# Softmax attention on one core: the values of a key tile in one piece of 512 queries, with both maxima and all scores between two pieces

## The chip, the cores and the metric

The kernel runs on one core of a Trainium2 chip. The metric is the device time of one execution in microseconds (us). Before the change it is 3828.96 us, the median of three runs (3827.2 to 3834.28). Engines are named as in the profile: PE is TensorE's matrix multiply, PEld its weight load, DVE is VectorE, ACT is ScalarE, POOL is GpSimd, SP is SyncE, which here only issues DMAs.

## The reference, cut to what matters

Two transformer layers on x of 2 x 2048 tokens by 256 channels. Each has a modulated layer norm, an attention and a mixture of experts. Two pieces are full softmax attentions over 2048 tokens with 16 heads of 16 channels, and they take two thirds of the time: the attention of layer 0, and the attention inside the second block of layer 1.

```
# layer 0 (q and k with rotary position, weights W_q, W_k, W_v)
scores = jnp.einsum('blhd,bshd->bhls', q, k) / math.sqrt(D_HEAD)
weights = jax.nn.softmax(scores, axis=-1)
out = jnp.einsum('bhls,bshd->blhd', weights, v).reshape(B, L, D_MODEL)
...
# layer 1, second block
attn = jnp.einsum('bqhd,bkhd->bhqk', q, k) / jnp.sqrt(jnp.asarray(hd, x.dtype))
attn = jax.nn.softmax(attn, axis=-1)
attn_out = jnp.einsum('bhqk,bkhd->bqhd', attn, v).reshape(B, S, D)
```

Everything else (projections, router and experts of layer 0, linear attention and experts of layer 1) is not touched.

## The kernel before

`softmax_attention` is called once in each layer. Both calls run the same program. The outer loop `it` goes over the two batches. Inside, `j` goes over 16 query blocks: four groups of four heads, times four blocks of 512 queries. Inside a block, `u` goes over 16 key tiles of 128 keys. So there are 2 x 2 x 16 = 64 query blocks and 64 x 16 = 1,024 key tiles in all.

In a key tile four kinds of work meet.

- Scores (L758): for each head h = 0 to 3 of the group one matmul makes the scores of 128 keys (output partitions) by 512 queries. Head h uses rows 0 to 63 or 64 to 127 of the array, so two heads' matmuls run side by side. The result goes to one of three PSUM banks (`SB = 3`), taken in turn over all scores.
- Exponentials (L823): ScalarE takes each bank to `probs`, which has two buffers by the parity of u. One instruction a head.
- Values (L772): four heads' matmuls, 17 columns of weights each (16 channels and a column of ones for the sum), at output partitions 32h. They add into one PSUM bank, `o_ps`, over the 16 tiles. A matmul in full fp32 appears in the trace as two passes, so four matmuls are eight records. They work one tile behind the scores: in tile u the values of u - 1 are made.
- Maxima (L740 and L844): the softmax is shifted by the row maximum, which needs scores with queries on the partitions. TensorE makes these for the next query block (eight tiles ahead, `LEAD`), two units a tile. A unit is a pair of matmuls, 128 queries by 1024 keys, into one of two PSUM slots (`max_ps`); VectorE reduces it with one instruction (L844). I call the two units of a tile M0 and M1.

The order on TensorE is written out by hand. A tile is two equal rounds: the first half of the values (queries 0 to 255), scores h = 2 and 3, M0; then the second half of the values, the next tile's scores h = 0 and 1, M1. TensorE waits at these places:

- scores c wait until exponential c - 3 is done (L756: `exp_done` at c - SB + 1), because they use its bank;
- a unit of maxima waits until the reduction of the unit two before it is done (L736: `slot_taken`);
- the first half of the values waits for the four exponentials of its tile (L764), and for u = 0 also for VectorE to have turned the result of the last query block out of `o_ps` (L766: `o_copied`).

VectorE, in its own hand-written order (L860 to L874), takes the maxima as they come. After the first unit of a block it turns the last block's result (`turn_result`, L849, a transpose out of `o_ps`, which waits for the last values of that block). After the first unit of tile 2 it divides (L853, L856). In tiles 8 and 9 it reduces and turns the row maxima (L381 to L394), which SyncE stores and loads as the shift of the next block.

The names and lines that the rest speaks of: scores L750 to L759, values L761 to L776, the tile's order L784 to L816, the exponentials L818 to L838, VectorE L840 to L875. TensorE, ScalarE, VectorE and SyncE are bound together by semaphores only.

Of the kernel before, what the change touches and what calls it, by code (L numbers as in the profile page):

```python
# [26 lines left out]
G = 512  # L27
TPG = G // P
GPB = T // G
KH = D // P  # L30
HG = 4
NHG = NH // HG
AUG = HD + 1
# [284 lines left out]
NB = GPB * NHG  # L318
LEAD = 8
MAXI = HG * TPG * 2  # L320
FIRST = MAXI + 2 * LEAD
# [23 lines left out]
def maximum_parts(k):  # L345

    return k // (TPG * GPB), k // GPB % TPG, k % GPB
# [249 lines left out]
NG = NHG  # L597
KT = TPB
# [7 lines left out]
def softmax_attention(nc, m, io, ai, tag, zero_slots=False, last=False):  # L606
# [5 lines left out]
    with ExitStack() as ctx:  # L612
        sb, pb, sem = allocators(ctx, nc, tag)
        q_sb, k_sb = ai.q, [ai.k[0], sb("k_sb1", [P, PAIRS, T], F32R)]
        v_sb = sb("v_sb", [P, 2, TPB, VROW])
        probs = sb("probs", [P, 2, HG, G])
# [20 lines left out]
        EXPS = KT * HG  # L637
        SLOTS_IT = NB * MAXI
# [84 lines left out]

        @block.tensor
        def _(pe):
            def maxima(used, r, j, k, it2):


                if k == 0:
                    pe.wait_ge(q_loaded[j % QR], NQ * (it2 * (NB // QR) + j // QR + 1))  # L730
                    if j % GPB == 0:
                        g = j // GPB
                        if g == 1:
                            pe.wait_ge(rows_set, 4)
                        pe.wait_ge(k_loaded[g % 2], NK * (it2 * (NG // 2) + g // 2 + 1))
                pe.wait_ge(slot_taken, used - 1)  # L736
                pair, tile, part = maximum_parts(k)
                for half in range(2):
                    rows = slice(half * HROWS, half * HROWS + XROWS)
                    last = nc.tensor.matmul(max_ps[:, r, half], q_sb[rows, j % QR, pair, tile * P:(tile + 1) * P],  # L740
                                            k_sb[j // GPB % 2][rows, pair, part * G:(part + 1) * G], start=True, stop=True)
                    if half == 0:
                        yield
                last.then_inc(slot_ready, 1)
                yield

            def scores(n, j, u, h, first=False):
                c = n * EXPS + u * HG + h
                if u == 0 and h == 0:
                    pe.wait_ge(shift_stored, NSH * (n + 1))  # L750
                if j == 0 and u == 0 and h < SB:

                    if h == 0 and not first:
                        pe.wait_ge(exp_done, n * EXPS)
                else:
                    pe.wait_ge(exp_done, c - SB + 1)  # L756
                pair, rows = h // 2, slice(h % 2 * HROWS, h % 2 * HROWS + XROWS)
                nc.tensor.matmul(s_ps[:, (j * EXPS + u * HG + h) % SB], k_sb[j // GPB % 2][rows, pair, u * P:(u + 1) * P],  # L758
                                 q_sb[rows, j % QR, pair], start=True, stop=True).then_inc(s_ready, 1)  # L759

            def values(n, j, u, it, part):  # L761

                if part == 0:
                    pe.wait_ge(exp_done, n * EXPS + (u + 1) * HG)  # L764
                    if u == 0:
                        pe.wait_ge(o_copied, n)  # L766
                        if j % GPB == 0:
                            g = j // GPB
                            pe.wait_ge(v_loaded[g % 2], 16 * (it * (NG // 2) + g // 2 + 1))
                cols = slice(part * (G // 2), (part + 1) * (G // 2))  # L770
                for h in range(HG):
                    last = nc.tensor.matmul(o_ps[32 * h:32 * h + AUG, cols], v_sb[:, j // GPB % 2, u, h * AUG:(h + 1) * AUG],  # L772
                                            probs[:, u % 2, h, cols], start=(u == 0 and part == 0), stop=(u == KT - 1),
                                            skip_group_check=True)
                if part == 1:
                    last.then_inc(pv_done, 1)  # L776

            pe.wait_ge(o_zeroed, 1)
            for h in range(2):
                scores(0, 0, 0, h, first=True)  # L780
            with pe.Fori(0, NIT) as it:
                for j in range(NB):
                    n = it * NB + j
                    for u in range(KT):  # L784

                        def ahead(i):
                            k, slot = 2 * (u + LEAD) + i, slot_of(j, u, i)
                            g = j + 1 + k // MAXI
                            return maxima(FIRST + it * SLOTS_IT + slot, slot % 2, g % NB, k % MAXI, it + g // NB)
# [7 lines left out]
                        def values_behind(part):  # L797

                            if u > 0:
                                values(n, j, u - 1, it, part)  # L800
                            elif j > 0:
                                values(n - 1, j - 1, KT - 1, it, part)

                        a, b = ahead(0), ahead(1)
                        values_behind(0)
                        scores(n, j, u, 2)
                        scores(n, j, u, 3)
                        next(a)
                        next(a)
                        values_behind(1)  # L810
                        next_scores(0)
                        next_scores(1)
                        next(b)
                        next(b)
                for part in range(2):
                    values(n, NB - 1, KT - 1, it, part)  # L816

        @block.scalar  # L818
        def _(act):
# [20 lines left out]
        @block.vector  # L840
        def _(dve):
            def max_take(used, r, j, k):
                dve.wait_ge(slot_ready, used + 1)  # L843
                nc.vector.reduce_max(part_max[:, j % 2, k], max_ps[:, r], AX.X).then_inc(slot_taken, 1)  # L844

            def turn_result(n):
                dve.wait_ge(pv_done, (n + 1) * KT)
                dve.wait_ge(o_ready, n)  # L848
                nc.vector.transpose(o_sb[:].rearrange("p k c -> p (k c)"), o_ps[:]).then_inc(o_copied, 1)  # L849

            def divide(n, j):
                dve.wait_ge(o_copied, n + 1)
                nc.vector.reciprocal(inv[:], o_sb[:, :, HD]).then_inc(inv_ready, 1)  # L853
                dve.wait_ge(inv_ready, n + 1)
                dve.wait_ge(o_stored, (n - 1 if j > 1 else n - j) * 16 * HG)
                nc.vector.tensor_tensor(o_div[:, j % 2], o_sb[:, :, 0:HD], inv[:].unsqueeze(2).broadcast_to([P, G // 32, HD]),  # L856
                                        ALU.mult).then_inc(o_ready, 1)

            nc.vector.memset(o_ps[:], 0.0).then_inc(o_zeroed, 1)  # L859
            with dve.Fori(0, NIT) as it:  # L860
                for j in range(NB):
                    n = it * NB + j
                    for u in range(KT):
                        for i in range(2):
                            k, slot = 2 * (u + LEAD) + i, slot_of(j, u, i)
                            max_take(FIRST + it * SLOTS_IT + slot, slot % 2, j + 1 + k // MAXI, k % MAXI)
                            if u >= KT - LEAD:
                                row_maxima(nc, dve, ai, n + 1, j + 1, k % MAXI, slots_until(it, j, KT - LEAD - 1, 1))
                            if j > 0 and u == 0 and i == 0:
                                turn_result(n - 1)  # L870
                            if j > 0 and u == RESULT_AT and i == 0:
                                divide(n - 1, j - 1)
                turn_result(n)
                divide(n, NB - 1)  # L874
            dve.wait_ge(slot_taken, FIRST + NIT * SLOTS_IT)  # L875
# [1099 lines left out]
```

## Time and profile before

| | |
|---|---|
| median of three runs | 3828.96 us |
| the profiled execution, its own time | 3825.79 us |
| its span | 3824.0 us |
| TensorE busy | 3496.8 us (91%) |
| VectorE busy | 3312.5 us (87%) |
| ScalarE busy | 2525.3 us (66%) |
| GpSimd busy | 253.1 us (7%) |
| clock granted to TensorE, mean | 0.953 of full speed |
| DMA, mean over the span | 53 GB/s |

The profile shows one execution. The shares of busy time are means over stages with different limits. The two attentions lie from about 215 to 1508 us and from about 2514 to 3806 us; nearly all of the maxima, exponentials, scores and values of the table of groups lie there. The start of a matmul record is the start of its weight load when that load was not hidden, and its end is modelled; two records can overlap. So the distance from one start to the next tells more than the length of a record. The clock is a share of 2.4 GHz: 1.00 is 2.4 GHz, 0.50 is 1.2 GHz.

### The profile page before, as it was taken

Reading aid. Unit: us, or ns where it says so; the run is one execution under the profiler, and the core shown is the slowest. Engines: PE = TensorE matmul, PEld = TensorE weight load, DVE = VectorE, ACT = ScalarE, POOL = GpSimd, SP = SyncE. Lnnn points to the kernel's source line nnn. Section 1 sums busy time; section 2 is a strip of 40 time slices with the busy share of each in tenths; the row PEclk is TensorE's granted clock in tenths of the full one; section 3 lists DMA queues with packets and bytes.
Section 4 is the critical chain, followed back from the end, with each engine's and each line's share of the span. In section 5 each row is a group of like instructions: output and inputs, shape, how many; then the busy total and the mean of one; then the engine's idle time right before and its main releaser. Section 6 shows DMA issues by size and latency. Waiting matters only on the chain. (4 is left out here: it accounts for less than half of the span.)

```text
span 3824.0 us, 89676 instructions
## 1 busy us (share of the span) xinstructions
PE 3496.8 (91%) x30116; PEld 1598.4 (42%) x30116; DVE 3312.5 (87%) x4392; ACT 2525.3 (66%) x4636; POOL 253.1 (7%) x211
## 2 busy tenths in 40 slices
PE   6889999999999998676888799889999999999997
PEld 4433333333333333565666577533333333333332
DVE  5989999999999997524666587899999999999997
ACT  2268888888888886232222223158888888888886
POOL 2210000000000000232210000000000010000001
PEclk8879999999999999898999899889999999999999
DMA  5840220202202022253000233220220212202021
GB/s 170 196 128 14 42 36 18 38 14 41 38 14 42 14 40 62 97 169 95 27 22 11 66 78 76 64 40 14 42 36 18 38 42 58 37 14 42 14 52 43
DMA packets 281193, 200.93 MB, mean 53 GB/s; under 512 B 203785, under 2 KB 234930, under 8 KB 275644
## 3 DMA queue, kind: packets, MB, share of 16 engines
q1 hardware_dynamic: 272300, 166.30, 20.3%
q0 software_dynamic: 8496, 29.43, 2.3%
q8 instruction: 237, 3.88, 0.4%
q14 instruction: 160, 1.31, 0.1%
HBM read 114.29 MB, written 81.82 MB: 51 GB/s over the span
## 5 line engine op out<-in xcount | busy, mean ns | idle before, releaser
L844 DVE TENSOR_REDUCE att_in_part_max<-att_l_max_ps 128x2 f32<-128x1024 f32 x2048 | 2447.3, 1218 | 50.5 <-PE att_l_max_ps L740 49.5
L823 ACT ACTIVATE att_l_probs<-att_l_s_ps 128x512 f32<-128x512 f32 x4096 | 2222.9, 595 | 345.9 <-PE att_l_s_ps L758 89.9
L772 PE MATMUL att_l_o_ps<-att_l_probs,att_l_v_sb 128*17 128x256 f32 x16384 | 1289.4, 387 | 49.1 <-DVE att_l_o_sb L849 39.2
L772 PEld LDWEIGHTS att_l_o_ps<-att_l_probs,att_l_v_sb 128*17 128x17 f32 x16384 | 273.7, 95 | 791.0 <-ACT att_l_probs L823 406.2
L758 PE MATMUL att_l_s_ps<-att_in_q_sb,att_in_k_sb 50*128 50x512 f32 x2052 | 522.0, 503 | 16.9 <-DVE att_l_o_ps L859 8.2
L758 PE MATMUL att_l_s_ps<-att_in_q_sb,att_l_k_sb 50*128 50x512 f32 x2048 | 511.7, 496 | 0.0
L740 PE MATMUL att_l_max_ps<-att_in_k_sb,att_in_q_sb 50*128 50x512 f32 x2048 | 414.7, 399 | 0.0
L740 PE MATMUL att_l_max_ps<-att_l_k_sb,att_in_q_sb 50*128 50x512 f32 x2048 | 403.4, 389 | 0.0
L758 PEld LDWEIGHTS att_l_s_ps<-att_in_q_sb,att_in_k_sb 50*128 50x128 f32 x2052 | 195.1, 185 | 459.9 <-ACT att_l_probs L823 438.2
L758 PEld LDWEIGHTS att_l_s_ps<-att_in_q_sb,att_l_k_sb 50*128 50x128 f32 x2048 | 190.6, 183 | 434.1 <-ACT att_l_probs L823 434.1
L740 PEld LDWEIGHTS att_l_max_ps<-att_in_k_sb,att_in_q_sb 50*128 50x128 f32 x2048 | 197.3, 189 | 2.0
L740 PEld LDWEIGHTS att_l_max_ps<-att_l_k_sb,att_in_q_sb 50*128 50x128 f32 x2048 | 193.9, 186 | 3.1 <-issue 0.7
L1859 DVE SCALAR_TENSOR_TENSOR ffn_acc<-ffn_qk_ps,ffn_comb,ffn_acc 128x256 f32<-128x256 f32 x256 | 123.9, 484 | 32.8 <-PE ffn_qk_ps L1768 25.2
L1356 DVE TENSOR_TENSOR post_hid<-post_act_gate,post_zT_ps 128x256 f32<-128x256 f32 x32 | 13.5, 421 | 105.5 <-ACT post_act_gate L1252 105.5
L1768 PE MATMUL ffn_qk_ps<-ffn_w_hi,ffn_h_hi 128*128 128x512 f32 x256 | 102.4, 400 | 0.0
L717 POOL TENSOR_TENSOR att<-att,all_gates 128x1024 f32<-128x1024 f32 x8 | 18.9, 2365 | 1249.7 <-DMA att<-att_rows 1249.7
L1768 PE MATMUL ffn_qk_ps<-ffn_w_hi,ffn_h_lo 128*128 128x512 f32 x256 | 101.3, 396 | 0.0
L1768 PE MATMUL ffn_qk_ps<-ffn_w_lo,ffn_h_hi 128*128 128x512 f32 x256 | 101.0, 394 | 0.0
L1626 DVE TENSOR_TENSOR lin_masked<-lin_qk_ps,all_triu 128x1024 f32<-128x1024 f32 x64 | 75.0, 1213 | 24.4 <-PE lin_qk_ps L1463 24.4
L1245 ACT ACTIVATE post_slot_hT<-post_y_ps,all_modv 128x256 f32<-128x256 f32 x64 | 32.6, 560 | 85.9 <-PE post_y_ps L1149 85.8
L823 ACT ACT_TABLE_LOAD x4 | 5.1, 1283 | 121.9 <-PEq L71 118.6
L1558 ACT ACTIVATE lin_o_sb<-lin_o_ps 128x512 f32<-128x512 f32 x32 | 19.1, 597 | 98.5 <-PE lin_o_ps L1472 98.5
(218 smaller groups left out, 2791.4 us busy)
## 6 DMA issues: line engine op xcount, KB each, us to landing
att_in_q_sb<-q_hi SPq DMA_DIRECT2D x280, 64.0 KB
att_in_k_sb<-k_hi SPq DMA_DIRECT2D x40, 256.0 KB, 9.4
att_in_q_sb<-q_lo SPq DMA_DIRECT2D x140, 72.0 KB
att_l_v_sb<-v_rows SPq DMA_DIRECT2D x18, 544.0 KB, 14.0
att_l_k_sb<-k_hi SPq DMA_DIRECT2D x32, 256.0 KB, 9.1
slot_rows<-att_l_zeros POOLq DMA_DIRECT2D x8, 1024.0 KB, 13.9
att_rows<-att_l_o_div SPq DMA_DIRECT2D x256, 32.0 KB, 1.8
post_rows<-slot_rows SPq DMA_DIRECT2D x32, 256.0 KB, 2.9
```

The costliest lines, as they stand in the source:

```text
L717: nc.gpsimd.tensor_tensor(att, att, gate, ALU.mult).then_inc(att_scaled, 1)
L740: last = nc.tensor.matmul(max_ps[:, r, half], q_sb[rows, j % QR, pair, tile * P:(tile + 1) * P], k_sb[j // GPB % 2][rows, pair, part * G:( ...
L758: nc.tensor.matmul(s_ps[:, (j * EXPS + u * HG + h) % SB], k_sb[j // GPB % 2][rows, pair, u * P:(u + 1) * P], q_sb[rows, j % QR, pair], sta ...
L772: last = nc.tensor.matmul(o_ps[32 * h:32 * h + AUG, cols], v_sb[:, j // GPB % 2, u, h * AUG:(h + 1) * AUG], probs[:, u % 2, h, cols], star ...
L823: nc.scalar.activation(probs[:, u % 2, h], s_ps[:, (j * EXPS + u * HG + h) % SB], ACT.Exp, scale=float(HD) ** -0.5).then_inc(exp_done, 1)
L844: nc.vector.reduce_max(part_max[:, j % 2, k], max_ps[:, r], AX.X).then_inc(slot_taken, 1)
L1245: nc.scalar.activation(slot_hT[:, i % 2, half], rT_ps[:, i % 2, half], ACT.Identity, bias=m.modv[:, 0, 2, half, b:b + 1], scale=m.modv[:, ...
L1356: nc.vector.tensor_tensor(hid[:, i % 2], act_gate[:, i % 2], gf_ps[:, i % 2, 1], ALU.mult).then_inc(hid_ready, 1)
L1558: nc.scalar.activation(o_sb[:], o_ps[:], ACT.Copy).then_inc(o_copied, 1)
L1626: nc.vector.tensor_tensor(masked[:, t % 2, banks].rearrange("p r e n -> p (r e) n"), qk_ps[:, banks].rearrange("p r (e n) -> p (r e) n", n=P),
L1768: last = nc.tensor.matmul(qk_ps[:, pair], h[:, slot * KH + kh, t * P:(t + 1) * P], w[:, kh, pair * 2 * D:(pair + 1) * 2 * D], start=(kh == ...
L1859: nc.vector.scalar_tensor_tensor(acc[:, t], qk_ps[:, e // 2, (e % 2) * D:(e % 2 + 1) * D], comb[:, t, e:e + 1], acc[:, t], ALU.mult, ALU.a ...
```

## The change

On TensorE the tile has one round instead of two. The values of the tile before are made in one piece of 512 queries: four matmuls instead of two times four. The order is scores h = 2 and 3; values; next tile's scores h = 0 and 1; M0; M1. So both maxima and all four scores stand between two pieces of values. The start flag of the accumulation is on the one piece now. The generator that issued a unit of maxima in two steps becomes a plain function.

On VectorE `turn_result` goes ahead of the first unit of maxima of a block instead of behind it. Everything else stays: the three score banks, the two slots, the number of instructions on ScalarE and VectorE, the DMAs and what the waits ask for.

```diff
-            def values(n, j, u, it, part):
-
-                if part == 0:
-                    pe.wait_ge(exp_done, n * EXPS + (u + 1) * HG)
...
-                cols = slice(part * (G // 2), (part + 1) * (G // 2))
+            def values(n, j, u, it):
+                pe.wait_ge(exp_done, n * EXPS + (u + 1) * HG)
+                if u == 0:
+                    pe.wait_ge(o_copied, n)
...
                 for h in range(HG):
-                    last = nc.tensor.matmul(o_ps[32 * h:32 * h + AUG, cols], v_sb[:, j // GPB % 2, u, h * AUG:(h + 1) * AUG],
-                                            probs[:, u % 2, h, cols], start=(u == 0 and part == 0), stop=(u == KT - 1),
-                                            skip_group_check=True)
-                if part == 1:
-                    last.then_inc(pv_done, 1)
+                    last = nc.tensor.matmul(o_ps[32 * h:32 * h + AUG], v_sb[:, j // GPB % 2, u, h * AUG:(h + 1) * AUG],
+                                            probs[:, u % 2, h], start=(u == 0), stop=(u == KT - 1))
+                last.then_inc(pv_done, 1)
...
-                        a, b = ahead(0), ahead(1)
-                        values_behind(0)
                         scores(n, j, u, 2)
                         scores(n, j, u, 3)
-                        next(a)
-                        next(a)
-                        values_behind(1)
+                        if u > 0:
+                            values(n, j, u - 1, it)
+                        elif j > 0:
+                            values(n - 1, j - 1, KT - 1, it)
                         next_scores(0)
                         next_scores(1)
-                        next(b)
-                        next(b)
-                for part in range(2):
-                    values(n, NB - 1, KT - 1, it, part)
+                        for i in range(2):
+                            maxima(i)
+                values(n, NB - 1, KT - 1, it)
...
+                            if j > 0 and u == 0 and i == 0:
+                                turn_result(n - 1)
                             max_take(FIRST + it * SLOTS_IT + slot, slot % 2, j + 1 + k // MAXI, k % MAXI)
                             if u >= KT - LEAD:
                                 row_maxima(nc, dve, ai, n + 1, j + 1, k % MAXI, slots_until(it, j, KT - LEAD - 1, 1))
-                            if j > 0 and u == 0 and i == 0:
-                                turn_result(n - 1)
```

The instructions of TensorE for one key tile in the middle of a block, before, from one first half of the values on: `o_ps` is the result, `s_ps` the scores, `max_ps` the maxima; 17x256 is one head's values.

```order
L772 MATMUL att_l_o_ps<-att_l_probs,att_l_v_sb 17x256 x4
L758 MATMUL att_l_s_ps<-att_in_q_sb,att_in_k_sb 128x512
L756 REGISTER_ALU
L758 MATMUL att_l_s_ps<-att_in_q_sb,att_in_k_sb 128x512
L736 REGISTER_ALU
L740 MATMUL att_l_max_ps<-att_in_k_sb,att_in_q_sb 128x512 x2
L772 MATMUL att_l_o_ps<-att_l_probs,att_l_v_sb 17x256 x4
L756 REGISTER_ALU
L758 MATMUL att_l_s_ps<-att_in_q_sb,att_in_k_sb 128x512
L756 REGISTER_ALU
L758 MATMUL att_l_s_ps<-att_in_q_sb,att_in_k_sb 128x512
```

The same place after:

```order
L740 MATMUL att_l_max_ps<-att_in_k_sb,att_in_q_sb 128x512 x2
L753 REGISTER_ALU
L755 MATMUL att_l_s_ps<-att_in_q_sb,att_in_k_sb 128x512
L753 REGISTER_ALU
L755 MATMUL att_l_s_ps<-att_in_q_sb,att_in_k_sb 128x512
L766 MATMUL att_l_o_ps<-att_l_probs,att_l_v_sb 17x512 x4
L753 REGISTER_ALU
L755 MATMUL att_l_s_ps<-att_in_q_sb,att_in_k_sb 128x512
L753 REGISTER_ALU
L755 MATMUL att_l_s_ps<-att_in_q_sb,att_in_k_sb 128x512
L736 REGISTER_ALU
L740 MATMUL att_l_max_ps<-att_in_k_sb,att_in_q_sb 128x512 x2
```

In the second list the scores h = 2 and 3 (the first two rows of L755) follow a pair of maxima, the four value matmuls of 512 columns follow them, and the next scores h = 0 and 1 stand ahead of the maxima. The halves of the values are gone from between scores h = 0 and 1 and scores h = 2 and 3.

The instructions of VectorE where one block ends and the next begins, before: the reduction is a unit of maxima, the transpose is the turn of the result.

```order
L844 TENSOR_REDUCE att_in_part_max<-att_l_max_ps 128x2
L843 REGISTER_ALU
L844 TENSOR_REDUCE att_in_part_max<-att_l_max_ps 128x2
L847 REGISTER_ALU
L849 STREAM_TRANSPOSE att_l_o_sb<-att_l_o_ps 128x512
L843 REGISTER_ALU
L844 TENSOR_REDUCE att_in_part_max<-att_l_max_ps 128x2
```

After:

```order
L830 TENSOR_REDUCE att_in_part_max<-att_l_max_ps 128x2
L829 REGISTER_ALU
L830 TENSOR_REDUCE att_in_part_max<-att_l_max_ps 128x2
L833 REGISTER_ALU
L835 STREAM_TRANSPOSE att_l_o_sb<-att_l_o_ps 128x512
L829 REGISTER_ALU
L830 TENSOR_REDUCE att_in_part_max<-att_l_max_ps 128x2
```

The transpose stood behind the first reduction of the new block; now it stands ahead of it.

## Rows read from the trace of the kernel before

**Rows 1.** Busy time of each engine in attention stretches (windows; us, then busy and count)

```profile
core 0: us, PE busy (x) PEld busy (x) DVE busy (x) ACT busy (x) POOL busy (x), PEclk, DMA share, GB/s
300.00:800.00 500.00, 489.35 (x4816) 174.39 (x4812) 493.53 (x501) 435.06 (x802) 0.00 (x0) 1.00 0.17 29
...
3200.00:3700.00 500.00, 489.36 (x4816) 174.44 (x4812) 493.51 (x501) 435.05 (x802) 0.00 (x0) 1.00 0.17 29
```

**Rows 2.** Groups by line; busy us, mean ns, idle us before and its releaser

```profile
L844 DVE TENSOR_REDUCE att_in_part_max<-att_l_max_ps 128x2 f32<-128x1024 f32 x2048 | 2447.3, 1218 | 50.5 <-PE att_l_max_ps L740 49.5
...
L772 PE MATMUL att_l_o_ps<-att_l_probs,att_l_v_sb 128*17 128x256 f32 x16384 | 1289.4, 387 | 49.1 <-DVE att_l_o_sb L849 39.2 <-ACT att_l_probs L823 9.9
...
L849 DVE STREAM_TRANSPOSE att_l_o_sb<-att_l_o_ps 128x512 f32<-128x512 f32 x64 | 45.1, 705 | 0.0
```

**Rows 3.** Timeline, TensorE, one undisturbed round; start us, us, engine, line

```profile
1038.93 0.62 PE L772 MATMUL att_l_o_ps<-att_l_probs,att_l_v_sb 128*17 128x256 f32 x8
...
1039.49 0.50 PE L758 MATMUL att_l_s_ps<-att_in_q_sb,att_l_k_sb 50*128 50x512 f32 x2
...
1039.83 0.40 PE L740 MATMUL att_l_max_ps<-att_l_k_sb,att_in_q_sb 50*128 50x512 f32 x2
...
1040.15 0.63 PE L772 MATMUL att_l_o_ps<-att_l_probs,att_l_v_sb 128*17 128x256 f32 x8
```

**Rows 4.** Timeline, VectorE, division and the reductions behind it

```profile
1035.30 0.24 DVE L853 RECIPROCAL att_l_inv<-att_l_o_sb 128x16 f32<-128x16 f32 x1
...
1036.02 4.61 DVE L844 TENSOR_REDUCE att_in_part_max<-att_l_max_ps 128x2 f32<-128x1024 f32 x4
```

**Rows 5.** Timeline, all engines, around a turn of the result

```profile
1029.60 0.70 DVE L849 STREAM_TRANSPOSE att_l_o_sb<-att_l_o_ps 128x512 f32<-128x512 f32 x1
...
1030.41 0.62 PE L772 MATMUL att_l_o_ps<-att_l_probs,att_l_v_sb 128*17 128x256 f32 x8 [0.78 <-ACT att_l_probs L823]
...
1030.96 0.50 PE L758 MATMUL att_l_s_ps<-att_in_q_sb,att_l_k_sb 50*128 50x512 f32 x2
...
1031.30 0.39 PE L740 MATMUL att_l_max_ps<-att_l_k_sb,att_in_q_sb 50*128 50x512 f32 x2
...
1031.50 1.08 ACT L823 ACTIVATE att_l_probs<-att_l_s_ps 128x512 f32<-128x512 f32 x2 [0.98 <-PE att_l_s_ps L758]
...
1031.73 1.22 DVE L844 TENSOR_REDUCE att_in_part_max<-att_l_max_ps 128x2 f32<-128x1024 f32 x1 [0.32 <-PE att_l_max_ps L740]
```

**Rows 6.** Chain of waits, two turns, one query block apart; start us, us

```profile
2719.15 0.71 DVE att_l_o_sb L849
...
2759.02 0.71 DVE att_l_o_sb L849
```

**Rows 7.** Timeline, TensorE, matmuls of 512 and of 256 columns (projection)

```profile
94.76 6.60 PE L581 MATMUL qkv_qk_ps<-qkv_ln_hT,qkv_w_qk 128*128 128x512 f32 x15
...
102.08 3.62 PE L588 MATMUL qkv_v_ps<-qkv_w_v,qkv_ln_hT 128*128 128x256 f32 x16
```

**Rows 8.** Instructions of three lines; duration ns min/median/max, first and last start

```profile
L823 ACT ACTIVATE att_l_probs<-att_l_s_ps x4096: 592/597/618, 216.7 to 3800.6; 128x512 f32<-128x512 f32 x196
...
L758 PE MATMUL att_l_s_ps<-att_in_q_sb,att_in_k_sb x2052: 387/497/793, 215.9 to 3801.3; 50*128 50x512 f32 x187
...
L740 PE MATMUL att_l_max_ps<-att_l_k_sb,att_in_q_sb x2048: 383/386/502, 323.2 to 3741.6; 50*128 50x512 f32 x187
```

**Rows 9.** Timeline, start of the second attention, all engines

```profile
2515.55 1.57 ACT L823 ACTIVATE att_l_probs<-att_l_s_ps 128x512 f32<-128x512 f32 x3
...
2516.20 0.79 PE L758 MATMUL att_l_s_ps<-att_in_q_sb,att_in_k_sb 50*128 50x512 f32 x1 [0.26 <-ACT att_l_probs L823]
```

**Rows 10.** Windows of the first maxima of layer 1 (line L362)

```profile
2460.00:2470.00 10.00, 7.15 (x18) 2.59 (x18) 10.00 (x9) 0.00 (x0) 0.00 (x0) 0.50 0.00 0
```

**Rows 11.** Timeline, TensorE, second attention, clock at half

```profile
2520.46 1.05 PE L772 MATMUL att_l_o_ps<-att_l_probs,att_l_v_sb 128*17 128x256 f32 x8
...
2522.60 0.96 PE L772 MATMUL att_l_o_ps<-att_l_probs,att_l_v_sb 128*17 128x256 f32 x8
```

More of the change, by code:

```diff
@@ L725, in _, with maximum @@
         def _(pe):
-            def maxima(used, r, j, k, it2):
+            def maximum(used, r, j, k, it2):
                 if k == 0:
@@ L741, in maxima @@
                                             k_sb[j // GPB % 2][rows, pair, part * G:(part + 1) * G], start=True, stop=True)
-                    if half == 0:
-                        yield
                 last.then_inc(slot_ready, 1)
-                yield
             def scores(n, j, u, h, first=False):
@@ L759, in scores @@
                                  q_sb[rows, j % QR, pair], start=True, stop=True).then_inc(s_ready, 1)
-            def values(n, j, u, it, part):
-                if part == 0:
-                    pe.wait_ge(exp_done, n * EXPS + (u + 1) * HG)
[L765 to L769, printed above, removed]
-                cols = slice(part * (G // 2), (part + 1) * (G // 2))
-                for h in range(HG):
-                    last = nc.tensor.matmul(o_ps[32 * h:32 * h + AUG, cols], v_sb[:, j // GPB % 2, u, h * AUG:(h + 1) * AUG],
-                                            probs[:, u % 2, h, cols], start=(u == 0 and part == 0), stop=(u == KT - 1),
-                                            skip_group_check=True)
-                if part == 1:
-                    last.then_inc(pv_done, 1)
+            def values(n, j, u, it):
+                pe.wait_ge(exp_done, n * EXPS + (u + 1) * HG)
+                if u == 0:
+                    pe.wait_ge(o_copied, n)
+                    if j % GPB == 0:
+                        g = j // GPB
+                        pe.wait_ge(v_loaded[g % 2], 16 * (it * (NG // 2) + g // 2 + 1))
+                for h in range(HG):
+                    last = nc.tensor.matmul(o_ps[32 * h:32 * h + AUG], v_sb[:, j // GPB % 2, u, h * AUG:(h + 1) * AUG],
+                                            probs[:, u % 2, h], start=(u == 0), stop=(u == KT - 1))
+                last.then_inc(pv_done, 1)
             pe.wait_ge(o_zeroed, 1)
@@ L784, in _, with maxima @@
                     for u in range(KT):
-                        def ahead(i):
+                        def maxima(i):
                             k, slot = 2 * (u + LEAD) + i, slot_of(j, u, i)
                             g = j + 1 + k // MAXI
-                            return maxima(FIRST + it * SLOTS_IT + slot, slot % 2, g % NB, k % MAXI, it + g // NB)
+                            maximum(FIRST + it * SLOTS_IT + slot, slot % 2, g % NB, k % MAXI, it + g // NB)
                         def next_scores(h):
@@ L795, in next_scores @@
                                 scores(n + 1, (j + 1) % NB, 0, h)
[L797 to L802, printed above, removed]
-                        a, b = ahead(0), ahead(1)
-                        values_behind(0)
                         scores(n, j, u, 2)
                         scores(n, j, u, 3)
-                        next(a)
-                        next(a)
-                        values_behind(1)
+                        if u > 0:
+                            values(n, j, u - 1, it)
+                        elif j > 0:
+                            values(n - 1, j - 1, KT - 1, it)
                         next_scores(0)
                         next_scores(1)
-                        next(b)
-                        next(b)
-                for part in range(2):
-                    values(n, NB - 1, KT - 1, it, part)
+                        for i in range(2):
+                            maxima(i)
+                values(n, NB - 1, KT - 1, it)
         @block.scalar
```

## The prediction

> **What bounds the kernel now.** I began with the clock and the busy time by engine. Inside both attention stages the clock is granted in full (1.00), TensorE is busy 98% of the time and VectorE 99% [rows 1]. Which of two full engines is the bound can't be told by their shares. So I went to the groups by line: the maxima on VectorE (L844) have 50 us of idle before them over 2,048 instructions, the values (L772) 49 us, so neither waits much [rows 2]. Then the timeline of a stretch without disturbance [rows 3]. TensorE repeats values, scores, maxima every 1.22 us: values at 1038.93, again at 1040.15. A key tile is two such rounds, 2.44 us. The steps in a round are values to scores 0.56, scores to maxima 0.335 (0.34 in the row), maxima to values 1.22 - 0.56 - 0.335 = 0.33.
>
> VectorE can go faster than that. After its reciprocal and division it catches up: four reductions in 4.61 us, with 1.22 for the last, are (4.61 - 1.22) / 3 = 1.13 us apart [rows 4]. ScalarE too: after a wait two exponentials cover 1.08 us, so the second starts 0.49 us after the first (1.08 less 0.59), about 2 us for a tile of four [rows 5]. So TensorE's own sequence is the bound in the undisturbed tile, and VectorE follows 7% below it.
>
> A query block (16 key tiles) takes 39.87 us between two turns of the result (L849) [rows 6]. 32 rounds of 1.22 are 39.04; the other 0.83 is the turn itself. There TensorE stands 0.78 us until VectorE has turned the old result, because the first values of the next block are at the front of the tile [rows 5]; the row puts the wait down to ScalarE, but the turn ended last, at 1029.60 + 0.70 = 1030.30. There are 64 such blocks in the two layers (64 turns in [rows 2]).
>
> **What the change takes off TensorE.** The eight value matmuls in two pieces of 256 columns become four of 512. Each is run in two passes. A pass of full precision costs (6.60 - 0.59) / 14 = 0.43 us for 512 columns and (3.62 - 0.38) / 15 = 0.22 us for 256 [rows 7], so the columns cost what they did: 0.21 more for each of two passes. Saved is what lies between kinds. Values to scores becomes 0.56 + 0.43 = 0.98, once. Scores to maxima stays 0.335. The steps maxima to maxima and maxima to scores have the weights loaded behind the matmul before them: 0.335 less the 0.11 by which a score matmul (0.497) is longer than a maximum matmul (0.386) [rows 8] is 0.23 each. Scores to values is 0.33, as maxima to values was. The sum is 0.98 + 0.335 + 0.23 + 0.23 + 0.33 = 2.10 us a tile against 2.44. If nothing waited, VectorE would be the next bound.
>
> The Trainium skill (TensorEngine Tiling (Array Packing), Key Properties) says that a change of tiling mode drains TensorE. The steps of [rows 3] agree: about 0.1 us more at each change of kind. By that rule alone the tile gains, since it has two changes instead of four; this is the fourth rival below.
>
> **What the change adds: a longer ring of waits.** There are three score banks for four heads. So the fourth scores of a tile, h=3, write the bank that exponential h=0 of the same tile has to have read (L756). The scores h=0 of a tile are issued in the tile before. In the old order one half of the values stood between scores h=3 and the next scores h=0, the other half between scores h=0 and scores h=3. Now nothing but maxima stands between h=0 and h=3, and the whole of the values between h=3 and the next h=0. The ring, from one scores h=0 to the next:
> - scores h=0 start to exponential h=0 start: 1030.96 to 1031.50, 0.535 us [rows 5];
> - the exponential: 0.597 us (median) [rows 8];
> - its end to the weights of the waiting scores: 2515.55 + 0.60 = 2516.15, scores at 2516.20: 0.05 us [rows 9];
> - scores h=3, which now load their weights after the wait and not behind another matmul, to values: 0.33 + 0.11 = 0.435;
> - values to scores h=0: 0.98.
>
> That is 2.60 us a tile, of which 1.18 us pass from h=0 to h=3, where TensorE needs only 0.335 + 0.23 + 0.23 = 0.80. TensorE so stands about 0.4 us in each tile. In the old order the same ring closes in a round: 0.535 + 0.597 + 0.05 = 1.18 against the 1.22 that TensorE takes from one pair of scores to the next: 0.04 us of cover, and the change takes it.
>
> Is anything later than 2.60? VectorE needs 2 x 1.13 = 2.26. Its two slots: M0 starts 0.335 after scores h=0; its reduction starts 0.43 later (1031.30 to 1031.73, [rows 5]), at 0.77; the second at 1.90, and ends at 3.12 with the 1.22 us of L844. The next M1 can start at 3.12 + 0.05 = 3.17, if VectorE is heard as soon as ScalarE is. That is 0.57 after the next scores h=0 at 2.60. It may be as late as 1.18 - 0.335 = 0.84 without holding scores h=3. So there is 0.27 us of slack in each tile.
>
> **Once in a block.** The turn now goes ahead of the first maxima on VectorE and waits for the last values of the block. These start at 1.18 + 0.435 = 1.61 after scores h=0, and the second pass ends about 1.0 later, at 2.65, while VectorE has maxima to reduce until 1.90 + 1.13 = 3.03. The turn takes 0.70 us, to 3.74; the values that need the empty bank come at 1.61 + 2.60 = 4.21. So the 0.83 us of the turn are gone. The turn makes the maxima later by 0.3 us, about the slack, at no cost. Reciprocal and division hold VectorE 0.72 us (1035.30 to 1036.02) [rows 4]. The old order hid them in the 7%. Now M1 of the tile is 0.72 later where 0.27 is free: scores are held by 0.44, less 0.11 since h=2 and h=3 then go together: 0.34 us. The row maxima come in pieces of 0.1 to 0.2 us and fit in the slack. Queries, keys and the shift are asked for a block ahead, and there are no more of their DMAs than before.
>
> The ring's sum to three places is 2.597, so a block is 16 x 2.597 + 0.34 = 41.89 us against 39.87: 2.02 us more, times 64 = 129 us. On the profiled execution (3825.8 us, span 3824.0) that is 3955. The median of the runs is 3 us above that execution, which I leave in the range.
>
> **Bounds of the uncertain step.** No row shows scores h=3 alone after a wait with values behind. If its weight load costs nothing there (0.33 instead of 0.435, the row of maxima to values), the tile is 2.49 us, the block 40.2, the kernel 3848 us. Upward: if the two passes of 512 columns lose as much at their start as scores do (0.11 once more), the tile is 2.70 and the block 43.5: 4060 us. I take the middle, since the 0.11 is measured on the same matmul in the same form after a change of kind.
>
> **Rivals.**
> 1. The hidden load, just worked out: 3848 us. For it speaks that TensorE loads weights behind a running matmul elsewhere; against it, that the wait sits at the load (the weight rows name ScalarE). 13%.
> 2. Later still, 2.70 or more: a second wait in the tile (M1 late after every reduction), or the clock. With two maxima pairs per 2.26 us alone, the stage before the attention ran at 0.50 ([rows 10], ten us of it). The attention keeps its columns and spreads them over 6% more time, so I expect 1.00. At half clock a round takes 2.13 us ([rows 11], 2520.46 to 2522.60); if the clock fell for a tenth of the 1,024 tiles, at some 1.5 us each, the cost is 150 us more. 12%, about 4060 us.
> 3. Not slower: the score ring isn't the last one to end, since h=3 finds its bank free sooner than I read from L756. Then the two slots decide: M1 to scores 0.335, to values 0.33, to scores 0.98, to M0 0.335, to its reduction 0.43, 1.13 to the second, 1.22 to its end, 0.05 to M1: 4.81 us for two tiles, 2.40 each. With about 1 us of turn, division and row maxima a block takes 39.4: 3826 - 64 x 0.5 = 3794 us. It decides if the ring of scores closes in under 2.40 us. For it: VectorE is fuller than ScalarE now. Against it: the index in L756 and L758 leaves no fourth bank. 8%.
> 4. The drains are saved and nothing waits: VectorE at 1.13 us, 32 x 1.13 + 1.9 (0.63 to 0.72 for turn and for division, about 0.6 for the row maxima) = 38.1 a block: 3712 us. It needs both rings open. 5%.
>
> **How the numbers follow.** 62% for the forecast (3925 to 3985 us, a tile of 2.57 to 2.64), 13%, 12%, 8% and 5% for the rivals. The range reaches down to the hidden load, 3840, and up to 4020, between the forecast and the second rival's 4060; outside it are the two faster cases and about half of the second rival, 19% together. A change under 0.2%, about 8 us, can't be told from none: 4% (the third rival when its extras are dearer). Faster 10%, slower 86%.
>
> **What would show it.** In the timeline after: 2.60 us from values to values; scores h=3 alone, 0.3 to 0.4 us behind h=2 where the two started together, at 0.05 after the end of exponential h=0 (the record of h=2 covers most of that wait, so TensorE may still look busy); values 0.43 after h=3, and scores 0.98 after values; reductions alternating 1.13 and 1.47 us; VectorE busy about 90%, ScalarE about 80%; no wait of values for the turn; 41.9 us between turns; clock 1.00. I am wrong if scores h=2 and h=3 still start together in the undisturbed tile, or if the gap stands at M1 instead, with the slot as its releaser.

## The result and the profile after

The change makes the kernel slower. The median goes from 3830.15 us (3827.2 to 3834.28) to 3945.15 us (3944.44 to 3947.08), four runs each: a ratio of 1.030, 95% interval 1.0282 to 1.0318. The forecast was 3955 us. The profiled execution took 3945.16 us, its span is 3943.4 (before 3824.0), and the mean clock 0.955 (before 0.953). So 119.4 us were added to the span, where 129 were forecast.

The busy time by engine inside the two attentions (windows; columns as in [rows 1]):

```profile
core 0: us, PE busy (x) PEld busy (x) DVE busy (x) ACT busy (x) POOL busy (x), PEclk, DMA share, GB/s
300.00:800.00 500.00, 490.95 (x3062) 172.75 (x3065) 467.56 (x480) 398.16 (x766) 0.00 (x0) 1.00 0.17 28
3200.00:3700.00 500.00, 488.79 (x3040) 172.11 (x3038) 464.41 (x477) 396.39 (x761) 16.66 (x9) 1.00 0.18 34
```

The clock is full as before. VectorE fell from 99% to 93%, ScalarE from 87% to 80%. TensorE still reads 98%, and that figure misleads: it hides the new wait. The groups by line show where it stands (columns as in [rows 2]):

```profile
L830 DVE TENSOR_REDUCE att_in_part_max<-att_l_max_ps 128x2 f32<-128x1024 f32 x2048 | 2418.1, 1218 | 186.5 <-PE att_l_max_ps L740 184.2
...
L809 ACT ACTIVATE att_l_probs<-att_l_s_ps 128x512 f32<-128x512 f32 x4096 | 2130.0, 602 | 550.8 <-PE att_l_s_ps L755 549.6
...
L766 PE MATMUL att_l_o_ps<-att_l_probs,att_l_v_sb 128*17 128x512 f32 x8192 | 1083.1, 601 | 0.0
```

The reductions idled 50.5 us before and idle 186.5 now, waiting for TensorE. The values waited 49.1 us, 39.2 of it for the turn (L849), and now 0.0. VectorE is therefore not the bound, and the turn no longer is either. What TensorE waits for shows in its weight loads. One tile on all engines (timeline; start us, us, then in brackets the idle time and its releaser):

```profile
1043.70 0.50 PE L755 MATMUL att_l_s_ps<-att_in_q_sb,att_in_k_sb 50*128 50x512 f32 x2
...
1044.04 0.83 PE L740 MATMUL att_l_max_ps<-att_l_k_sb,att_in_q_sb 50*128 50x512 f32 x4
...
1044.23 2.06 ACT L809 ACTIVATE att_l_probs<-att_l_s_ps 128x512 f32<-128x512 f32 x4 [0.51 <-PE att_l_s_ps L755]
...
1044.71 0.67 PE L755 MATMUL att_l_s_ps<-att_in_q_sb,att_in_k_sb 50*128 50x512 f32 x2
1044.88 0.18 PEld L755 LDWEIGHTS att_l_s_ps<-att_in_q_sb,att_in_k_sb 50*128 50x128 f32 x1 [0.22 <-ACT att_l_probs L809]
...
1045.31 1.05 PE L766 MATMUL att_l_o_ps<-att_l_probs,att_l_v_sb 128*17 128x512 f32 x8
...
1046.29 0.51 PE L755 MATMUL att_l_s_ps<-att_in_q_sb,att_in_k_sb 50*128 50x512 f32 x2
```

Read it as a ring. Scores h = 0 start at 1043.70, their exponential at 1044.23. With 0.597 us it ends at 1044.83. The load of scores h = 3 starts at 1044.88, released by that exponential. Values follow at 1045.31, the next scores h = 0 at 1046.29: 2.59 us around. The second L755 row says two matmuls in 0.67 us; they are h = 2 at 1044.71 and, with its load, h = 3 at 1044.88. The 0.17 us between them lie inside that one record, so TensorE seems busy. In [rows 3] the two start together, in 0.50 us.

This tile stands right behind the row maxima, which hold VectorE. In the tile behind it, with no extra work, scores h = 3 start 0.25 us behind h = 2, as in most tiles (0.247 in the median). M1 too waits there, for its slot (timeline; the first row is the load of M1):

```profile
1046.88 0.19 PEld L740 LDWEIGHTS att_l_max_ps<-att_l_k_sb,att_in_q_sb 50*128 50x128 f32 x2 [0.29 <-DVE att_in_part_max L830]
...
1047.22 0.75 PE L755 MATMUL att_l_s_ps<-att_in_q_sb,att_in_k_sb 50*128 50x512 f32 x2
1047.47 0.18 PEld L755 LDWEIGHTS att_l_s_ps<-att_in_q_sb,att_in_k_sb 50*128 50x128 f32 x1 [0.30 <-ACT att_l_probs L809]
```

M1's wait ends early enough; the wait of scores h = 3 is the one that ends last.

The turn and the division on VectorE (timeline), over two blocks:

```profile
1017.86 0.70 DVE L835 STREAM_TRANSPOSE att_l_o_sb<-att_l_o_ps 128x512 f32<-128x512 f32 x1
...
1018.49 4.65 DVE L830 TENSOR_REDUCE att_in_part_max<-att_l_max_ps 128x2 f32<-128x1024 f32 x4
...
1024.53 0.24 DVE L839 RECIPROCAL att_l_inv<-att_l_o_sb 128x16 f32<-128x16 f32 x1
...
1059.70 0.71 DVE L835 STREAM_TRANSPOSE att_l_o_sb<-att_l_o_ps 128x512 f32<-128x512 f32 x1
```

The turn ends at 1018.56, and the values that need the empty bank start at 1019.02, as late after scores h = 3 as in any tile. That answers to [rows 5], where TensorE stood 0.78 us. From turn to turn it is 41.84 us here, and 41.81 in the median, against 39.87 in [rows 6] (39.89 in the median of the kernel before).

### The profile page after: what moved, and what is told of

It is laid out like the page before. It is cut to its first block and busy times, and to the rows that moved or that the text cites. A ratio compares the mean times of both kernels' runs of the same rounds, so it can differ in the third digit from the quotient of the medians.

```text
span 3943.4 us, 73290 instructions
## 1 busy us (share of the span) xinstructions
PE 3619.3 (92%) x21922; PEld 1633.6 (41%) x21924; DVE 3290.9 (83%) x4392; ACT 2432.7 (62%) x4636; POOL 253.1 (6%) x211
## 3 DMA queue, kind: packets, MB, share of 16 engines
q8 instruction: 173, 2.83, 0.3%
## 5 line engine op out<-in xcount | busy, mean ns | idle before, releaser
L830 DVE TENSOR_REDUCE att_in_part_max<-att_l_max_ps 128x2 f32<-128x1024 f32 x2048 | 2418.1, 1218 | 186.5 <-PE att_l_max_ps L740 184.2
L809 ACT ACTIVATE att_l_probs<-att_l_s_ps 128x512 f32<-128x512 f32 x4096 | 2130.0, 602 | 550.8 <-PE att_l_s_ps L755 549.6
L766 PE MATMUL att_l_o_ps<-att_l_probs,att_l_v_sb 128*17 128x512 f32 x8192 | 1083.1, 601 | 0.0
L755 PE MATMUL att_l_s_ps<-att_in_q_sb,att_in_k_sb 50*128 50x512 f32 x2052 | 617.1, 472 | 14.7 <-DVE att_l_o_ps L845 8.2
L755 PE MATMUL att_l_s_ps<-att_in_q_sb,att_l_k_sb 50*128 50x512 f32 x2048 | 608.3, 467 | 0.0
L755 PEld LDWEIGHTS att_l_s_ps<-att_in_q_sb,att_in_k_sb 50*128 50x128 f32 x2052 | 286.0, 186 | 581.2 <-ACT att_l_probs L809 552.8
L755 PEld LDWEIGHTS att_l_s_ps<-att_in_q_sb,att_l_k_sb 50*128 50x128 f32 x2048 | 281.4, 184 | 558.3 <-ACT att_l_probs L809 553.9
L740 PEld LDWEIGHTS att_l_max_ps<-att_in_k_sb,att_in_q_sb 50*128 50x128 f32 x2048 | 194.7, 186 | 186.5 <-DVE att_in_part_max L830 185.5
L766 PEld LDWEIGHTS att_l_o_ps<-att_l_probs,att_l_v_sb 128*17 128x17 f32 x8192 | 136.0, 95 | 252.1 <-issue 131.0
L809 ACT ACT_TABLE_LOAD x4 | 5.1, 1283 | 123.1 <-PEq L71 119.4
```

The costliest lines, as they stand in the source:

```text
L766: last = nc.tensor.matmul(o_ps[32 * h:32 * h + AUG], v_sb[:, j // GPB % 2, u, h * AUG:(h + 1) * AUG], probs[:, u % 2, h], start=(u == 0), ...
L809: nc.scalar.activation(probs[:, u % 2, h], s_ps[:, (j * EXPS + u * HG + h) % SB], ACT.Exp, scale=float(HD) ** -0.5).then_inc(exp_done, 1)
```

## Experiments

Each kernel is compared with the kernel before on the same chip. On the chips of e1 to e4, e9 and e10 the kernel before took 3903 to 3904 us, on the chip of e5 to e8 3829.82. The difference lies between the two attentions and not in them: from the first matmul behind the first attention to the first of layer 1's second block it is 689 us in e1 and in e9, 616 in the trace of before. So ratios are compared, or times of one chip. "Block" is the time between two turns at full clock. Experiments with "old" change the kernel before, those with "new" the kernel after.

### The ring of scores: e4 and e3, a fourth score bank

```diff
-SB = 3
+SB = 4
-        max_ps = pb("max_ps", [P, 2, 2, G])
+        max_ps = pb("max_ps", [P, 3, G])
...
+                    if r == 1 and half == 1:
+                        continue
+                    out = max_ps[:, half] if r == 0 else max_ps[:, 2]
```

The first two lines are in e3 alone. In both kernels VectorE also reads the lone bank twice, and the exponent's scale is a quarter.

> The control for the run before: the same second unit of maxima with one matmul, the bank read twice, and the scale of a quarter, but three score banks. Theory: 2.59 us a tile as in the changed kernel, 3945 us. Rival (the lone matmul or the other bank layout is itself faster or slower): another time, and by so much the run with four banks has to be corrected.

> The changed order with four score banks instead of three. The bank is taken from the maxima: the second unit of a tile makes one head's scores alone (one matmul instead of a pair side by side, the same time on TensorE), VectorE reads that bank twice (the same 1024 elements), and the other head's row maxima leave out these keys; the exponent's scale is a quarter. Theory (the ring of three banks is the bound of the changed tile): the ring opens, scores h=2 and 3 start together again, and the next bound is the two slots of the maxima at 2.40 us a tile: a block of about 39.4 us instead of 41.8, 64 x 2.4 = 154 us less, 3790 us. Rival (what costs is the one long piece of values or the matmuls alone after a wait, not the bank): 3945 us. Rival (nothing else waits): VectorE's 2.26 us a tile, about 38.1 a block, 3710 us.

e4: 4011.7 us, ratio 1.0275 (1.0249 to 1.0301), block 41.78. The narrowed maxima alone leave tile and block as they were. e3: 3898.7 us, ratio 0.9986 (0.9975 to 0.9996), block 39.96. TensorE in e3 (timeline):

```profile
1043.90 1.05 PE L771 MATMUL att_l_o_ps<-att_l_probs,att_l_v_sb 128*17 128x512 f32 x8
...
1045.80 0.50 PE L745 MATMUL att_l_max_ps<-att_l_k_sb,att_in_q_sb 50*128 50x512 f32 x1 [0.19 <-DVE att_in_part_max L835]
1045.99 0.52 PE L760 MATMUL att_l_s_ps<-att_in_q_sb,att_l_k_sb 50*128 50x512 f32 x2
1046.45 1.05 PE L771 MATMUL att_l_o_ps<-att_l_probs,att_l_v_sb 128*17 128x512 f32 x8
...
1048.72 1.05 PE L771 MATMUL att_l_o_ps<-att_l_probs,att_l_v_sb 128*17 128x512 f32 x8
```

Tiles are 2.55 and 2.27 us in turn, mean 2.41, and the wait stands at the maxima, with VectorE as releaser. The fourth bank takes 1.82 us from each block, 116 in 64, and 113 us from the kernel. So the three banks are the cost of the change. The size was missed: I expected 154 us. The tile came as the slots' ring said (2.40), but the block's extras are larger: where the slots bind, VectorE has no slack for its extra work. The tile of the division takes 3.28 us, the one of the turn 2.81.

### The ring's length: e6 and e7, shorter exponentials

```diff
+            nc.vector.memset(probs[:], 1.0).then_inc(probs_set, 1)
...
-                nc.scalar.activation(probs[:, u % 2, h], s_ps[:, (j * EXPS + u * HG + h) % SB], ACT.Exp,
+                nc.scalar.activation(probs[:, u % 2, h, 0:384], s_ps[:, (j * EXPS + u * HG + h) % SB, 0:384], ACT.Exp,
```

> The changed kernel with exponentials of 384 of the 512 queries; the other 128 are ones, set once by VectorE ahead of each attention (some 4 us each). Exponentials of 512 start 0.49 us apart, so 128 columns less are 0.12 us less. Theory (one exponential lies in the ring of every tile): a tile of 2.59 - 0.12 = 2.47 us, a block 1.9 us shorter, 64 x 1.9 = 123 us less, plus 8 for setting the ones: 3830 us. Rival (ScalarE has time to spare at 80% busy, and the ring is closed by something else): 3945 to 3953 us.

> The order before the change with exponentials of 384 of the 512 queries, the rest ones as in the run before. Theory (bound by TensorE's own sequence, with 0.04 us between it and the ring): nothing but the setting of the ones, 3830 to 3840 us. Rival (the ring is the bound of the old order too): up to 0.12 us a round until VectorE's 1.13 us stops it, 0.09 x 32 x 64 = 180 us less, 3650 to 3700 us.

e6: 3872.59 us, ratio 1.0103 (1.0076 to 1.013). Exponentials are 0.11 us closer, and the tile is 2.48 us (1048.81 to 1051.29 below) against 2.59. In the old order (e7) the round stays 1.22 us, the block 39.89, the ratio 1.0023 (1.001 to 1.0036), some 12 us that I put down to setting the buffers. So ScalarE's length is in the path after the change and not before it. The block of e6 is 40.61, a gain of 1.20 where 1.9 was expected. The missing part is in tiles behind VectorE's extra work (timeline, TensorE, the tile of the division):

```profile
1045.74 1.05 PE L767 MATMUL att_l_o_ps<-att_l_probs,att_l_v_sb 128*17 128x512 f32 x8
...
1048.14 0.50 PE L741 MATMUL att_l_max_ps<-att_l_k_sb,att_in_q_sb 50*128 50x512 f32 x2 [0.69 <-DVE att_in_part_max L832]
...
1048.81 1.05 PE L767 MATMUL att_l_o_ps<-att_l_probs,att_l_v_sb 128*17 128x512 f32 x8
...
1051.29 1.05 PE L767 MATMUL att_l_o_ps<-att_l_probs,att_l_v_sb 128*17 128x512 f32 x8
```

This tile takes 3.07 us where it took 2.95, and its wait is at the slot. The tile behind the turn takes 2.72 where it took 2.59. The slots are close behind the ring of scores, less than 0.2 us a tile (2.59 against the 2.41 of e3).

### The ring's contents: e8, M0 ahead of the values

```diff
                         scores(n, j, u, 3)
+                        maxima(0)
                         if u > 0:
                             values(n, j, u - 1, it)
...
-                        for i in range(2):
-                            maxima(i)
+                        maxima(1)
```

> The changed order with the first unit of maxima moved from behind the scores h=0 and 1 to between scores h=3 and the values. TensorE's instructions are the same. Theory (only the part from scores h=3 to the next scores h=0 is in the ring, the part from h=0 to h=3 has 0.4 us to spare): the moved unit costs its 0.23 us in full: 2.82 us a tile, 3.7 us a block, 64 x 3.7 = 236 us more, 4180 us. Rival (what counts is the amount of work and of changes of kind in a tile, which stays): 3945 us.

4201.71 us, ratio 1.0962 (1.0925 to 1.0998), block 45.78, 3.97 more than after (3.7 expected). TensorE does the same matmuls; one pair was only moved from a stretch in which it waits (h = 0 to h = 3) to the stretch in which the ring waits for it. In the timeline of TensorE:

```profile
1043.93 1.05 PE L766 MATMUL att_l_o_ps<-att_l_probs,att_l_v_sb 128*17 128x512 f32 x8
...
1045.48 0.39 PE L755 MATMUL att_l_s_ps<-att_in_q_sb,att_in_k_sb 50*128 50x512 f32 x1
1046.10 0.49 PE L755 MATMUL att_l_s_ps<-att_in_q_sb,att_in_k_sb 50*128 50x512 f32 x1 [0.22 <-ACT att_l_probs L809]
1046.19 0.64 PE L740 MATMUL att_l_max_ps<-att_in_k_sb,att_in_q_sb 50*128 50x512 f32 x2
1046.76 1.05 PE L766 MATMUL att_l_o_ps<-att_l_probs,att_l_v_sb 128*17 128x512 f32 x8
```

Scores h = 3 now stand 0.62 us behind h = 2, and the tile is 2.83 us, 0.24 more than 2.59 (2.82 in the median). 16 x 0.23 are the 3.7 us expected. The rest changed places: the tile of the division takes no more than the others, but behind the turn one takes 3.43 us. VectorE now stands 0.96 us for the last values before it can turn, its next reduction is late, and M0, which is ahead of the values here, waits for the slot.

### The turn: e1, e2 and e9

e1 moves the turn in the kernel before; e2 moves it back in the kernel after; e9 is e1 with the division at tile 7.

```diff
+                            if j > 0 and u == 0 and i == 0:
+                                turn_result(n - 1)
                             max_take(FIRST + it * SLOTS_IT + slot, slot % 2, j + 1 + k // MAXI, k % MAXI)
...
-                            if j > 0 and u == 0 and i == 0:
-                                turn_result(n - 1)
...
-RESULT_AT = 2
+RESULT_AT = 7
```

The last two lines are in e9 alone.

> The order of TensorE before the change, with the VectorE part of the change alone: the turn of the result ahead of the first maxima of a block. Theory (the old order is bound by TensorE's own sequence of 1.22 us a round, and 0.83 us of each block is the turn): the turn now starts when the last values end, about 0.65 us after their second half starts, and the next values wait 0.2 us for it instead of 0.83; VectorE stands until then and takes its maxima late, which costs some 0.2 to 0.3 us at the slots. 0.3 to 0.4 us less a block, times 64: 3805 to 3812 us. Rival (what VectorE loses by standing is all paid again at the slots): 3830 us, unchanged.

3896.78 us, ratio 0.9986 (0.9973 to 0.9998), block 39.85: less than half of the least that I expected (5 to 8 us, against 17). VectorE and TensorE at the turn:

```profile
1064.74 0.72 DVE L849 STREAM_TRANSPOSE att_l_o_sb<-att_l_o_ps 128x512 f32<-128x512 f32 x1 [0.57 <-PE att_l_o_ps L772]
```

```profile
1064.94 0.40 PE L740 MATMUL att_l_max_ps<-att_l_k_sb,att_in_q_sb 50*128 50x512 f32 x2
1065.60 0.63 PE L772 MATMUL att_l_o_ps<-att_l_probs,att_l_v_sb 128*17 128x256 f32 x8 [0.27 <-DVE att_l_o_sb L849]
...
1066.62 0.50 PE L740 MATMUL att_l_max_ps<-att_l_k_sb,att_in_q_sb 50*128 50x512 f32 x2
1067.05 0.63 PE L772 MATMUL att_l_o_ps<-att_l_probs,att_l_v_sb 128*17 128x256 f32 x8
...
1068.26 0.63 PE L772 MATMUL att_l_o_ps<-att_l_probs,att_l_v_sb 128*17 128x256 f32 x8
```

Last maxima to values is 0.66 us here and in most turns, and 1.21 in most turns before, so the wait does fall by 0.55. But VectorE stands 0.57 us in front of the turn and is late for the slots. The round behind the turn takes 1.45 us (1065.60 to 1067.05, and in most turns) and the one with the division 1.49, where 1.22 is usual. The two give back 0.50.

> The order of TensorE before the change, the turn ahead of the first maxima (as in the first run), and the division in tile 7 of a block instead of tile 2. Theory (the turn makes VectorE late, it catches up by 1.22 - 1.13 = 0.09 us a round, and in tile 2, after four rounds, the 0.72 us of the division still meet the slots: the round there was 1.49 instead of 1.22): in tile 7 VectorE has caught up by 14 x 0.09 = 1.3 us, and the division costs nothing. 0.27 us a block less than the first run's 39.85, that is 39.58, and 0.3 less than the kernel before: 64 x 0.3 = 20 us less, a ratio to the kernel before of 0.995. Rival (VectorE has no time to catch up, and the division costs its 0.27 us wherever it stands): a ratio of 0.9986 as in the first run.

3885.0 us, ratio 0.9951 (0.9934 to 0.9967), block 39.58. With five tiles more in between VectorE has caught up before the division, and that round is back at 1.22. The block says 64 x (39.87 - 39.58) = 19 us, and the medians differ by 18. This is the fastest version found, below both kernels. The division at tile 7 without the move of the turn was not run.

> The changed order of TensorE with the turn back behind the first maxima of a block. Theory: the turn then starts one reduction later (4.49 us after the scores h=0 of the new block's first tile), ends at 5.20, and the values that need the empty bank, due at 4.20, wait 1.05 us; times 64 is 67 us more than the changed kernel: 4012 us, and the waits list shows values waiting for the turn. Rival (a block has slack for it, since TensorE stands in each tile anyway): 3945 us.

4125.57 us, ratio 1.0567 (1.0533 to 1.06). The values at a turn start 1.55 us after scores h = 3 instead of 0.43, so the wait is 1.13 us, near the 1.05 forecast. The blocks at full clock are 43.00 us in the median and 42.94 at the short end, which is 41.81 + 1.13: 72 to 76 us in 64. But on the same chip it is 114 us above e4, whose blocks are those of the changed kernel, and not the 67 expected. The other 40 or so go with the clock (windows of e2, from a turn on):

```profile
1090.00:1098.00 8.00, 6.96 (x46) 2.42 (x44) 7.35 (x7) 6.11 (x12) 0.00 (x0) 0.99 0.48 98
1098.00:1104.00 6.00, 6.00 (x26) 2.64 (x23) 2.67 (x3) 2.57 (x5) 0.00 (x0) 0.50 0.99 116
1104.00:1110.00 6.00, 5.38 (x36) 1.95 (x34) 5.61 (x7) 4.60 (x10) 0.00 (x0) 0.95 0.98 113
```

At about 30 of the turns the granted clock fell to 0.50 for 3.4 to 6.8 us; at the others, with the same wait, it stayed. So the move of the turn is worth more in the new order than its 0.83 us of standing: without it the changed kernel would also lose clock.

### The clock: e5 and e10

e5 is the edit of e3 on the old order, e10 that of e4.

> The order before the change with four score banks (the second unit of maxima one matmul, its bank read twice, the other head's row maxima without these keys, the scale a quarter). Theory: in the old order the ring of three banks closes in 1.18 us under the 1.22 us of TensorE's own sequence, so a fourth bank gives nothing: 3830 us, a round still 1.22. Rival (the old order was bound by the ring all along, since scores start 0.09 us after an exponential ends in every round): a round falls towards VectorE's 1.13 us, a block to about 38.5, 3740 us.

> The order and the three score banks before the change, with the second unit of maxima of a tile as one matmul, its bank read twice and the scale of a quarter: the control for the old order with four banks, whose clock stood at half for most of the attention. Theory A (one matmul in place of two side by side leaves TensorE so much less to do that its clock falls, whatever the banks are): the clock falls to half here too, rounds of 2.13 us, 4900 to 5500 us. Theory B (the fall came with the fourth bank or with that chip): 3830 us at full clock, rounds of 1.22.

e5 took 5342 us (4987 to 5515, four runs), e10 5092.74 (5004 to 5181, two runs). Windows of e5:

```profile
300.00:700.00 400.00, 390.19 (x3682) 138.81 (x3678) 392.57 (x401) 347.15 (x641) 0.00 (x0) 1.00 0.16 27
1000.00:1800.00 800.00, 800.00 (x4317) 244.96 (x4313) 478.37 (x470) 406.80 (x751) 0.00 (x0) 0.50 0.10 16
```

While e5 has the full clock, its block is 39.76 us in the median (20 blocks) and the round 1.22: a fourth bank gives the old order next to nothing, as expected. For the rest the clock is at half for 246, 905 and 1724 us on end. With three banks and the same lone matmul (e10):

```profile
300.00:700.00 400.00, 400.00 (x2160) 122.60 (x2154) 239.15 (x234) 203.11 (x375) 0.00 (x0) 0.50 0.10 21
1000.00:1800.00 800.00, 798.13 (x4305) 244.81 (x4301) 477.64 (x469) 407.20 (x750) 0.00 (x0) 0.50 0.10 18
```

So the fall doesn't need the fourth bank. It comes with what both kernels share: M1 as one matmul instead of a pair on both halves of the array, its bank read twice, and the quarter scale. The three were not tried one by one; that the lone matmul does it is likely, not shown. The changed order has all three in e3 and e4 and keeps the full clock, and why is open.

## Why the prediction was right

- **The ring of scores.** Its five steps were forecast at 0.535, 0.597, 0.05, 0.435 and 0.98 us, and came at 0.53, 0.597, 0.05, 0.425 and 0.98: 2.59 against 2.60. e3 shows that it is this ring (a bank more and it is gone), e6 that ScalarE's part counts in full, e8 that TensorE's part does. That it did not bound the old order is shown by e7 and, while its clock is full, e5.
- **The uncertain step.** Scores h = 3 load their weights in the open: 0.42 to 0.43 us to the values, near the 0.435 taken and far from the 0.33 of the first rival. How long TensorE stands was forecast too high, at about 0.4 us, with h = 3 0.3 to 0.4 behind h = 2; it is 0.25. The work from h = 0 to h = 3 takes 0.93 us and not 0.80: M1 waits for its slot, and its own load is then in the open, so M1 to scores is 0.34 and not 0.23. This lies inside the 1.18 us of the ring, so the time came out right all the same. No part of the second rival came: M1's wait holds up nothing in the undisturbed tile, and the clock is 1.00.
- **The turn.** No wait of values for it is left, as forecast. e1 shows that the move alone would have brought almost nothing in the old order. It needs the slack that VectorE has in the new one, and the slack costs more than the turn.
- **The division.** It costs 0.37 us, not 0.34: 2.96 us in the tile with it.
- **The sum.** 15 x 2.59 + 2.96 = 41.81 us a block, against 41.89; 64 x (41.81 - 39.87) = 124 us, against 129. The span grew by 119.4. By the first matmuls of the stages, 56 of it are in the first attention (from its first scores to the next stage 1305 us, now 1361), 59 in layer 1's second block with the second, and 6 in between; the stages ahead are 2 shorter. So the attentions grew by some 9 us less than the blocks say. Part of that is clock: inside the two attentions it is at half for 46 us before and for 30 after. A round takes 2.13 us at half clock and 1.22 at full, so 16 us less of it give back about 7 us, by my estimate. The forecast left these stretches out. The rest is open.
- **Shares.** ScalarE at 80% as forecast; VectorE 93% where I had said about 90%: its records are 1.22 us long even where they start 1.13 apart, so two that follow closely overlap.
- **The third and fourth rival.** The slots' ring of the third rival exists, and e3 runs by it (2.41 for 2.40), but its "about 1 us" of extras was too small: 39.96 - 16 x 2.41 = 1.4 us. With it, all that the order could give with a fourth bank is 0.14%. For the fourth rival, VectorE alone, the slots would have to be opened too; nothing here tests it. The Trainium skill (TensorEngine Tiling (Array Packing), Key Properties) has a change of tiling mode drain TensorE. The trace agrees so far as 0.1 us more stands at such a change in [rows 3]. But M1 and scores h = 3, which change no mode, show the same 0.1 when their weight load follows a wait, so the runs don't tell a drain from a load in the open. Saving two of four changes a tile brought nothing, because TensorE waits out what it saved.

## What to carry to other kernels

When work on one engine is regrouped to save switches, write down each ring of waits through the buffers with the new distances, before counting the savings: with three banks for four heads the distance from h = 0 to h = 3 had 0.04 us of cover, and the regrouping spent it. The busy share won't show such a ring, since a record can cover the wait; the distance from one start to the next of the same line does. A wait that is moved is gone only if the engine that now waits earlier has slack for it (e1), and the next burst of extra work on that engine should stand far enough behind (e9).

## What was unexpected of the hardware

- The old order with one matmul instead of a pair in one of two rounds (and the two other changes of that edit) stood at the half clock for hundreds of us (e5, e10: 0.50 in the windows, kernel times of 4987 to 5515 us), while the changed order with the same edit stayed at 1.00.
- Standing 1.13 us at a turn (1.55 from scores h = 3 to values) was followed by 3.4 to 6.8 us at half clock at about 30 of 64 turns (e2), and not at the others. The kernel before stands 0.78 us there [rows 5], and its blocks kept 39.87 us.
- On two of the chips the stages between the attentions took 73 us more (689 against 616 us), in kernels that are alike there; the whole of before took 3904 against 3830 us. 36 us of it lie ahead of layer 1's linear attention (297 against 261 in e1) and 37 in it (392 against 355). There one repeated piece takes 48 us at a mean granted clock of 0.89 in e1, and 41 us at 0.96 in the trace of before. What makes the clock lower there is not shown, nor whether it is the cause.
